# A second copy of the chunk and two differences in PSUM, in the edge stage of a four-layer kernel

## What is computed

```python
p3 = ((1, 1), (1, 1)); p2 = ((1, 0), (1, 0))
b1 = _norm(0.5 * _corr(x, SOBEL_X, p3) + 0.5 * _corr(x, SOBEL_Y, p3))
b2 = _norm(0.5 * _corr(x, SCHARR_X, p3) + 0.5 * _corr(x, SCHARR_Y, p3))
b3 = _norm(_corr(x, LAPLACE3, p3))
b4 = _norm(0.5 * _corr(x, ROBERTS_X, p2) + 0.5 * _corr(x, ROBERTS_Y, p2))
b5 = _norm(0.5 * _corr(x, PREWITT_X, p3) + 0.5 * _corr(x, PREWITT_Y, p3))
y = maxpool2(conv3x3(concat([b1, b2, b3, b4, b5], axis=1), conv1_w, conv1_b))
...                       # the hourglass: six more convolutions, two more poolings, three deconvolutions
return orig * y
```

## Time and profile before

| | us |
|---|---|
| median of three runs | 21136.5 |
| lowest, highest | 21025.62, 21212.93 |
| the profiled execution | 21070.22 |
| its span | 21068.6 |

### The profile page before, as it was taken

How to read it: one execution, slowest core, us unless ns; L and a number is a source line. 1 busy time by engine, 2 the same in 40 slices (tenths; PEclk the granted TensorE clock), 3 DMA queues, 4 the chain that set the end, 5 groups by cost and what they waited for, 6 DMA issues and landing times. The chain is left out here.

```text
span 21068.6 us, 398582 instructions
## 1 busy us (share of the span) xinstructions
PE 16924.9 (80%) x141144; PEld 7118.2 (34%) x141144; DVE 14859.5 (71%) x15523; ACT 12935.7 (61%) x23178; POOL 10507.4 (50%) x6534
## 2 busy tenths in 40 slices
PE   6888888888853888888888849999999436668999
PEld 2333333333321222222222215555555212223444
DVE  8999999999942788888888836666656248882111
ACT  6989889989931666666666628878878013331111
POOL 5877777777710677777777720000000347771000
PEclk9999999999976999999999969989989768889999
DMA  2000000000045000000000041211111775552111
GB/s 73 12 12 11 12 12 11 12 12 11 12 122 138 17 18 18 18 18 18 17 18 18 16 91 25 37 36 34 34 36 33 190 184 109 108 106 53 43 43 40
DMA packets 1504668, 964.38 MB, mean 46 GB/s; under 512 B 761016, under 2 KB 1329824, under 8 KB 1492264
## 3 DMA queue, kind: packets, MB, share of 16 engines
q1 hardware_dynamic: 1358488, 732.04, 15.6%
q10 hardware_dynamic: 118480, 117.04, 2.2%
q0 software_dynamic: 26624, 100.67, 1.7%
HBM read 733.84 MB, written 215.64 MB: 45 GB/s over the span
## 5 line engine op out<-in xcount | busy, mean ns | idle before, releaser
L323 DVE TENSOR_TENSOR l_mx<-l_p_v,l_puN 128x2048 f32<-128x2048 f32 x2560 | 5637.0, 2278 | 154.2 <-PE l_p_s L538 141.7
L538 PE MATMUL l_p_s<-l_mx,l_w2z 128*32 128x512 f32 x32768 | 3838.2, 613 | 582.2 <-ACT l_mx L450 320.2
L343 POOL TENSOR_TENSOR l_mx<-l_pv,l_puP 128x2048 f32<-128x2048 f32 x1024 | 3715.6, 3645 | 326.8 <-PE l_p_s L538 321.1
L1249 DVE TENSOR_TENSOR_SCAN l1m_hs<-l1m_da,l1m_carry,l1m_pu 128x512 f32<-128x512 f32 x2304 | 2823.7, 1267 | 114.0 <-issue 12.6
L1907 ACT ACTIVATE l1d_ab<-l1d_pt 128x1024 f32<-128x1024 f32 x2304 | 2299.0, 1025 | 699.2 <-PE l1d_pt L1661 672.7
L1298 POOL TENSOR_TENSOR l1m_hc<-l1m_hs,l1m_cs 128x1024 f32<-128x1024 f32 x1152 | 2709.9, 2352 | 9.2 <-DVE l1m_hs L1249 5.7
L469 ACT ACTIVATE l_mx<-l_pv,l_puP 128x128 f32<-128x128 f32 x8192 | 2447.1, 394 | 0.8
L1785 DVE TENSOR_SCALAR l1d_hat<-l1d_ab 128x1024 f32<-128x1024 f32 x2304 | 1623.8, 705 | 803.6 <-ACT l1d_ab L1907 483.3
L538 PEld LDWEIGHTS l_p_s<-l_mx,l_w2z 128*32 128x32 f32 x32768 | 986.9, 112 | 3031.3 <-issue 1779.3
L1239 DVE TENSOR_TENSOR l1m_pu<-l1m_pu,l1m_bs 128x512 f32<-128x512 f32 x2304 | 1476.9, 687 | 746.7 <-PE l1m_pu L994 746.7
L450 ACT ACTIVATE l_mx<-l_mx 128x2048 f32<-128x2048 f32 x1024 | 1954.8, 1909 | 48.0 <-POOL l_mx L343 47.2
(11 more groups left out here) (336 smaller groups left out, 24604.5 us busy)
## 6 DMA issues: line engine op xcount, KB each, us to landing
n_xt<-x_after SPq DMA_DIRECT2D x48, 2048.0 KB
l3a_xs<-x_after SPq DMA_DIRECT2D x384, 256.0 KB, 5.2
l3a_xe<-x_after SPq DMA_DIRECT2D x480, 96.0 KB, 2.1
l1m_sq<-seq SPq DMA_DIRECT2D x256, 144.0 KB
n_xt<-in_x_dram SPq DMA_DIRECT2D x16, 2048.0 KB
l_xs<-in_x_dram SPq DMA_DIRECT2D x128, 256.0 KB, 2.8
x_after<-l_ot SPq DMA_DIRECT2D x128, 256.0 KB, 2.4
l1d_xr<-x_after POOLq DMA_DIRECT2D x32, 1024.0 KB, 10.0
```

The source lines that it names most:

```text
L323: v.tensor_tensor(mx[:, r % QB, :, :, :], columns.unsqueeze(1).broadcast_to([P, 4, G, P]), rows.broadcast_to([P, 4, G, P]), ALU.max).then_ ...
L343: g.tensor_tensor(mx[:, r % QB, :, :, :], pv[:, u, :, :].unsqueeze(1).broadcast_to([P, 4, G, P]), rows.broadcast_to([P, 4, G, P]), ALU.add ...
L538: ins = pe.matmul(p_s[R * q:R * (q + 1), 512 * u:512 * (u + 1)], w2z[:, 31 - r:63 - r], mx[:, r % QB, q, :, :].rearrange("p t v -> p (t v) ...
L1249: dve.tensor_tensor_scan(hs[:, p % 3, part, :], da[:, p % 3, part, :], pu[:, LC * bank:LC * (bank + 1)], carry[:, u, c:c + 1], ALU.mult, A ...
```

## The change

Five edits, all in `edges`:
- ACT writes a second copy `xq` of the normalised chunk into two PSUM banks (`second_copy`, one instruction of 128 x 780). It is issued in `squares(c)` for chunk c+1, between the wait for DVE's chunk c and the squares of c. There is one such buffer.
- `td` and `tf` become two PSUM banks. DVE's td, tf and to(2) take one input from `xq`, and to(0), to(1), to(4) one from `td` or `tf`. Of DVE's eight instructions per chunk t3 and to(3) still have two SBUF inputs.
- DVE's order in a chunk is now t3, to(3), then the wait for `xq_ready`, td, tf, to(2), to(0), to(1), to(4). td and tf stand behind the wait for POOL; before they stood ahead of it.
- The convolution has three banks instead of four (k % 3); `ps` becomes a part of bank `bb`. PE's waits are moved to match, and `total` also waits for the border to be copied out.
- DVE does three chunks before pool 0 instead of four, and chunk 7 after pool 4. `normalised` of chunk 0 of the image after is moved ahead of `squares(7)`.

```diff
-        td = m.sb("td", [P, CR, W])
-        tf = m.sb("tf", [P, CR, W])
-        pc = m.bank("pc", 4)
+        pc = m.bank("pc", 3)
         bb = m.bank("bb")
-        ps = m.bank("ps")
+        xq_banks = m.bank("xq", 2)
+        xq = xq_banks[:, 0:(CR + 2) * (W + 2)].rearrange("p (y x) -> p y x", x=W + 2)
+        td_bank = m.bank("td")
+        tf_bank = m.bank("tf")
+        ps = bb[:, 256:512]
...
+            def second_copy(n, u):
+                act.wait_ge(xn_ready, n + 1)
+                act.activation(xq, xn[:, u], ACT.Copy).then_inc(xq_ready, 1)
+
-            def squares(i, c):
+            def squares(i, c, last=False):
                 u = c % 2
                 act.wait_ge(dve_chunk, i * NB + (c + 1))
+                if not last:
+                    second_copy(i * NB + (c + 1), 1 - u)
                 for o in range(OPS):
...
-                    squares(b + 1, 7)
                     if two_follow:
                         normalised(b + 2, 0, u)
+                    squares(b + 1, 7, not two_follow)
+                    if two_follow:
                         normalised(b + 2, 1, u)
...
             def chunk(i, c):
+                qx = lambda dy, dx: xq[:, 1 + dy:1 + dy + CR, 1 + dx:1 + dx + W]
-                v.wait_ge(xn_ready, n + 1)
                 if not (isinstance(n, int) and n < 1):
                     v.wait_ge(dve_chunk, n)
-                v.tensor_tensor(td[:], px(1, 1), px(-1, -1), ALU.subtract)
-                v.tensor_tensor(tf[:], px(-1, 1), px(1, -1), ALU.subtract)
-                v.wait_ge(pool_chunk, n + 1)
-                v.tensor_tensor(t3[:], t1[:, u], t2[:, u], ALU.add).then_inc(dve_first, 1)
                 if not (isinstance(n, int) and n < 2):
                     v.wait_ge(sq_done, n - 1)
+                v.wait_ge(pool_chunk, n + 1)
+                v.tensor_tensor(t3[:], t1[:, u], t2[:, u], ALU.add)
                 v.scalar_tensor_tensor(out=to(3), in0=tp[:, u, 0:CR], ...)
+                v.wait_ge(xq_ready, n + 1)
+                v.tensor_tensor(td, qx(1, 1), px(-1, -1), ALU.subtract)
+                v.tensor_tensor(tf, qx(-1, 1), px(1, -1), ALU.subtract).then_inc(dve_first, 1)
                 v.wait_ge(dve_first, n + 1)
+                v.scalar_tensor_tensor(out=to(2), in0=qx(0, 0), scalar=-4.0, in1=t3[:], ...)
+                v.scalar_tensor_tensor(out=to(0), in0=td, scalar=1.0, in1=te[:, u], ...)
+                v.scalar_tensor_tensor(out=to(1), in0=td, scalar=0.6, in1=te[:, u], ...)
+                v.scalar_tensor_tensor(out=to(4), in0=tf, scalar=2.0, in1=tg[:, u], ...).then_inc(dve_chunk, 1)
...
-                    for c in range(4):
+                    for c in range(3):
                         chunk(b + 1, c)
                 for k in range(4):
                     pool(b, k)
                     if follows:
-                        chunk(b + 1, 4 + k)
+                        chunk(b + 1, 3 + k)
                 pool(b, 4)
                 if follows:
+                    chunk(b + 1, 7)
                     totals(b + 1)
...
-                pe.wait_ge(pool_done, b * NB + (k + 1))
+                pe.wait_ge(pool_done, b * NB + (k + 1 + (k < 2)))
```

More of the change, by code:

```diff
@@ L2036, in edges @@
         po = m.sb("po", [P, NB, W])
-        pc = m.bank("pc", 4)
+        pc = m.bank("pc", 3)
         bb = m.bank("bb")
-        ps = m.bank("ps")
+        xq_banks = m.bank("xq", 2)
+        xq = xq_banks[:, 0:(CR + 2) * (W + 2)].rearrange("p (y x) -> p y x", x=W + 2)
+        td_bank = m.bank("td")
+        tf_bank = m.bank("tf")
+        td = td_bank[:, :].rearrange("p (y x) -> p y x", x=W)
+        tf = tf_bank[:, :].rearrange("p (y x) -> p y x", x=W)
+        ps = bb[:, 256:512]
         names = ("w_load v_load zeroed g_ready xn_ready pool_first pool_chunk dve_first dve_chunk sq_done acc_ready sum_done chain dev_ready w_ready "
-                 "taps_summed sums_ready fixed conv_done border_done border_out replaced pool_done biased stored")
+                 "xq_ready taps_summed sums_ready fixed conv_done border_done border_out replaced pool_done biased stored")
         (w_load, v_load, zeroed, g_ready, xn_ready, pool_first, pool_chunk, dve_first, dve_chunk, sq_done, acc_ready, sum_done, chain, dev_ready, w_ready,
-         taps_summed, sums_ready, fixed, conv_done, border_done, border_out, replaced, pool_done, biased, stored) = (m.sem(n) for n in names.split())
+         xq_ready, taps_summed, sums_ready, fixed, conv_done, border_done, border_out, replaced, pool_done, biased, stored) = (m.sem(n) for n in names.split())
         xs_in = [m.sem(f"xs_in{k}") for k in range(NB)]
@@ L2182, in border @@
                 act.wait_ge(border_done, b + 1)
-                act.wait_ge(pool_done, b * NB + 4)
+                act.wait_ge(pool_done, b * NB + 3)
                 lefts = bb[:, 0:64].rearrange("p (s k r) -> p s k r", s=2, r=CR)
@@ L2221, in _ @@
             normalised(0, 0, 0)
+            second_copy(0, 0)
             normalised(0, 1, 0)
             for c in range(NB):
+                if c == NB - 1:
+                    normalised(1, 0, 1)
                 squares(0, c)
@@ L2267, in _ @@
             v.memset(xs[:, 1:H + 2, H + 2:H + 4], 0.0).then_inc(zeroed, 1)
-            v.memset(red[:, 0:1], 0.0).then_inc(pool_done, 4)
+            v.memset(red[:, 0:1], 0.0).then_inc(pool_done, 3)
             v.memset(red[:, 1:2], 0.0).then_inc(border_out, 1)
@@ L2292, in chunk @@
+                v.tensor_tensor(td, qx(1, 1), px(-1, -1), ALU.subtract)
+                v.tensor_tensor(tf, qx(-1, 1), px(1, -1), ALU.subtract).then_inc(dve_first, 1)
                 v.wait_ge(dve_first, n + 1)
-                v.scalar_tensor_tensor(out=to(0), in0=td[:], scalar=1.0, in1=te[:, u], op0=ALU.mult, op1=ALU.add, accum_out=acc[:, 0, c:c + 1])
-                v.scalar_tensor_tensor(out=to(1), in0=td[:], scalar=0.6, in1=te[:, u], op0=ALU.mult, op1=ALU.add, accum_out=acc[:, 1, c:c + 1])
@@ L2295, in chunk @@
-                v.scalar_tensor_tensor(out=to(2), in0=px(0, 0), scalar=-4.0, in1=t3[:], op0=ALU.mult, op1=ALU.add, accum_out=acc[:, 2, c:c + 1])
-                v.scalar_tensor_tensor(out=to(4), in0=tf[:], scalar=2.0, in1=tg[:, u], op0=ALU.mult, op1=ALU.add,
+                v.scalar_tensor_tensor(out=to(2), in0=qx(0, 0), scalar=-4.0, in1=t3[:], op0=ALU.mult, op1=ALU.add, accum_out=acc[:, 2, c:c + 1])
+                v.scalar_tensor_tensor(out=to(0), in0=td, scalar=1.0, in1=te[:, u], op0=ALU.mult, op1=ALU.add, accum_out=acc[:, 0, c:c + 1])
@@ L2297, in chunk @@
+                v.scalar_tensor_tensor(out=to(1), in0=td, scalar=0.6, in1=te[:, u], op0=ALU.mult, op1=ALU.add, accum_out=acc[:, 1, c:c + 1])
+                v.scalar_tensor_tensor(out=to(4), in0=tf, scalar=2.0, in1=tg[:, u], op0=ALU.mult, op1=ALU.add,
                                        accum_out=acc[:, 4, c:c + 1]).then_inc(dve_chunk, 1)
@@ L2330, in pool @@
             def pool(b, k):
-                bank = pc[:, 512 * (k % 4):512 * (k % 4 + 1)]
+                bank = pc[:, 512 * (k % 3):512 * (k % 3 + 1)]
                 v.wait_ge(conv_done, b * NB + (k + 1))
@@ L2365, in once @@
                 pool(b, 7)
-                v.wait_ge(pool_done, b * NB + NB + 4)
+                v.wait_ge(pool_done, b * NB + NB + 3)
                 v.wait_ge(stored, b * 64 + 64)
@@ L2406, in step @@
                         r, j = 16 * k + CR * g + by + 2, bx + 2
-                        ins = pe.matmul(pc[C * g:C * (g + 1), 512 * (k % 4):512 * (k % 4 + 1)], weight(u, n), xs[:, r:r + CR, j:j + W],
+                        ins = pe.matmul(pc[C * g:C * (g + 1), 512 * (k % 3):512 * (k % 3 + 1)], weight(u, n), xs[:, r:r + CR, j:j + W],
                                         start=n == 0, stop=n == len(rounds) - 1, tile_position=(0, C * g))
@@ L2443, in once @@
                 if follows:
+                    pe.wait_ge(border_out, b + 2)
                     total(b + 1)
```

1 line of the change is left out of this document (removed).

## The result

The changed kernel takes 20966.9 us (median of 20 runs) against 21134.3 us (20 runs of the kernel before). The ratio is 0.9933, with a 95% interval from 0.9905 to 0.9961. That is 142 us less by the ratio, 168 by the medians. The prediction was 134 less. One of the 20 runs was slow (24345 us) and is left out of the ratio.

What follows compares the result with a forecast made beforehand. The edge stage was taken as bound by a loop of waits, no engine full. A gain of 8.1 us in each of 15 periods plus 12 for image 0, about 134, gave 21002 us, range 20900 to 21125.

Steps and rivals of the forecast that it cites:

- two chunks: In the edge stage's loop through POOL, DVE and ACT, two chunks would take 20.2 us against 23.85.
- start of chunk 2, later by: Between totals and the next chunk 2, ACT's new copy ahead of squares(0) would cost 0.6 us on the mean.
- a PSUM operand frees DVE from POOL: DVE instructions with one PSUM operand would not wait for POOL: six per chunk at 0.61 us each, start to start.
- rival B: DVE is freed but POOL's chunk stays at 10.6 us: gain 13 us in all, 21124 us; chance 0.08.
- C: DVE's t3 and to(3) do not collide with POOL either: gain 185 us in all, 20952 us; chance 0.12.
- The copy: ACT's new write of the chunk into PSUM, on the chain of waits, was taken as 1.03 us.
- The 65 ns per instruction: Possible extra time of DVE's six PSUM-source instructions: 18 us in all, leaving a gain of some 115.
- That of the three banks: PE's idle 25 us ahead of total would cover the missing fourth convolution bank; uncovered, a step of 9.2 us.
- The cover by PE's steps 6 and 7: After totals, PE's 18.39 us hold the stretch, so weights ready 3 us earlier gain nothing.
- three signs of a wrong prediction: Six DVE instructions staying at 1.5 us or more; xq_ready wait beyond 0.2; totals to chunk 2 growing by over 1.
- A: PSUM does not free DVE; all eight instructions stand behind POOL: some 195 us slower, 21331 us; chance 0.06.
- D: A transfer or bank is late next, costing one PE step of 9.2 us per image: 21140 us; chance 0.08.

Runs made afterwards that it cites:

- four chunks: The changed kernel with four chunks before the first pooling, as before the change, three banks kept; edge stage 1787.9 us against 1787.2.

## Why the prediction was right

| term | predicted | measured |
|---|---|---|
| POOL, chunk 2 | 8.1 | 8.1 |
| DVE, chunk 2 | 6.1 | 6.3, handover included |
| ACT: copy, squares, normalise, handovers | 5.9 | 5.6 |
| two chunks | 20.2 | 19.99 and 19.85 |
| POOL, chunk 7 | 9.0 | 9.05 |
| DVE's chunk 7 and ACT to the sums | 9.3 | 9.14 |
| chunk 2 to the sums | 66.8 | 66.14 |
| start of chunk 2, later by | 0.6 | 0 and 0.9; 0.4 on the mean of 15 periods |
| gain per period | 8.1 | 9.02 |
| gain of image 0 | 12 | 12.8 |

The step on which all hung was that a PSUM operand frees DVE from POOL. It was taken from L323 and holds for instructions which that row did not show: a scalar_tensor_tensor with an accumulator, and PSUM as output. The run with all operands in SBUF shows it to be the cause. The time of the whole kernel alone would not have: its interval (82 to 201 us less) rules out rival B (13), but not C (185).

**Terms that were off.** The copy was put at 1.03 us, by the normalise that writes SBUF, and measured 0.82. It stands on the chain three times per image (chunks 2, 4 and 7), 0.6 us of the 0.9 by which the gain per period was underrated. Most of the rest is in the start of chunk 2, put 0.6 later and measured 0.4 later on the mean of 15 periods, where single ones lie between 3.9 earlier (the first) and 2.0 later. Over 15 periods this makes 135.3 us instead of 121.5, with image 0 148.3 in the stage. The whole kernel's ratio, 142 us, agrees with both within its interval.

**The PSUM source's extra time.** The 65 ns per instruction that were weighed beside the sum are not there: td and tf, which read and write PSUM, take 0.69 us, as t3 in SBUF does. As an estimate, t3's 0.69 with the extra cycles that the Trainium skill ("VectorE: DVE Perf Modes", the section on the TRN2 errata) gives a PSUM source would be 0.75.

**Covers.** That of the three banks held: they cost nothing in the old order (1936.1 against 1935.5), and in the new one PE still has over 20 us to wait for the sums. The cover by PE's steps 6 and 7 held too, but it is thinner than the prediction has it. Weights at 20.0 us behind the sums were 0.8 later than step 7, and at 17.7 they are 1.7 earlier; the run with the normalise moved back, with weights at 21.1, lost 0.9 us per image behind the sums.

**The signs.** Two of the three signs of a wrong prediction did show, the second in part. DVE waits for `xq_ready` by far more than 0.2 us, but only in chunk 1: 1.7 to 6.9 us in 14 of the 16 images, 69.8 us in all. And the time from `totals` to chunk 2 grew by more than 1 us in four of the 15 periods, though by 0.4 on the mean. Neither means what it was named for. The wait in chunk 1 is for a copy that stands on ACT behind the mirror copies, and POOL's next chunk comes later still; in the loop, from chunk 2 to 7, no such wait shows.

**Rivals.** A: its mechanism exists but needs both inputs in SBUF. (Its 12.4 us is not eight instructions at 1.69, which would be 13.5, but t3 at 0.61 and seven at 1.69.) B fell: POOL's chunks went to 8.1 where DVE made no such access. C did not come: t3 and to(3) collide as reckoned (to(3) 1.76 in even chunks, 0.68 in odd ones). D: no transfer or bank became late in the changed kernel; with normalise ahead of the squares the strip of chunk 2 did.

**The scatter.** The 66 us between the profiled execution and the median, left unexplained, fit what the traces show of the stage ahead. These are the eleven profiled executions of versions that all leave it alone, by the granted clock of the stretch 13200 to 16000:

| granted clock | the edge stage began at, us |
|---|---|
| 0.92 (td and tf in SBUF) | 17198 |
| 0.89 to 0.91 (five kernels, the one before among them) | 17230 to 17241 |
| 0.87 (copy made twice) | 17351 |
| 0.86 (t2 made by DVE) | 17261 |
| 0.84, 0.83 (four chunks; first normalise moved back) | 17393, 17360 |
| 0.78 (the changed kernel) | 17437 |

The order is not perfect (0.86, 0.83), so this one stretch is not all of it. The runs of the changed kernel, with its instructions the same each time, say it again: the twelve with a mean granted clock of 0.910 to 0.920 took 20843 to 20981 us, the seven with 0.897 to 0.903 took 21072 to 21148. That is argued from what goes together; nothing was run to change the clock. The clocks of the 20 runs of the kernel before are not on record, so it stays open how far the 142 us depend on them.

## What to carry to other kernels

Where DVE and POOL both work on float32 tensors in SBUF, look at the mean durations: a 0.69 that is 1.7 beside POOL points to a shared input path, and one input in PSUM was enough to leave it, even at the price of a copy by an idle engine. Price such an edit on the chain that closes the loop, not on busy time: DVE's busy time in the stage fell by 442 us (1549 to 1107), the stage by 148. And when a loop of waits has been shortened, write the chain down again: here an exchange of two groups of instructions on ACT, two differences moved ahead of a wait, and one addition moved from POOL to DVE took another 172.7 us off the stage, more than the change itself.

## What the runs showed of the hardware

- **DVE and POOL take turns.** With two SBUF inputs each, their instructions pass one for one: with all operands in SBUF, seven of DVE's (18232.78 to 18243.98) stand beside seven of POOL's (18232.28 to 18243.44). A DVE instruction of 512 columns goes from 0.69 us to between 1.5 and 1.8 (POOL's takes 1.04 to 1.28 alone), and a POOL one gains 0.45, less than DVE's 0.69. Beside the longer instructions of the weights (2.6 us each, 1568 columns) POOL's te takes 2.82 instead of 1.28, so the wait grows with the other's length. The Trainium skill says in "SBUF — State Buffer", "Who interferes with whom", that the port pair the two share is an exclusive lock; the traces agree in the main, and show that it changes hands with every instruction.
- **ACT writes 128 x 780 from SBUF to PSUM in 0.82 us**, and 128 x 768 from SBUF to SBUF in 1.02. The second has scale and bias from memory as well, so the difference isn't all the destination's. The Trainium skill ("ScalarE: Activation LUTs", "Step-by-step: what each stage is for") calls PSUM the faster destination; that agrees in sign.
- **A lower granted clock and a longer kernel go together.** The 19 runs of the changed kernel that enter the ratio lie 304 us apart, with the same instructions (20843 at 0.920, 21148 at 0.897), and the edge stage began up to 239 us later behind a stretch at 0.78 than behind one at 0.92. Both are more than this change is worth. A change of under 1% in another stage is then read from that stage's own length.
